# A graph network's attention ends: who weights the own rows, and where residual and bias are summed

## The reference

```
def gat_conv(x, src, dst, W, att_src, att_dst, bias, n_nodes):
    h = (x @ W).reshape(n_nodes, Hh, Cc)
    ...
    w = e / jnp.clip(denom, 1e-16)[dst]
    out = jax.ops.segment_sum(w[:, :, None] * h[src], dst, num_segments=n_nodes)
    return out.reshape(n_nodes, Hh * Cc) + bias
...
loops = jnp.arange(n, dtype=edge_index.dtype)
src = jnp.concatenate([edge_index[0], loops])
dst = jnp.concatenate([edge_index[1], loops])
h1 = gat_conv(x, src, dst, W1, att_src1, att_dst1, b1, n)
h1 = jax.nn.relu(h1)
out = gat_conv(h1, src, dst, W2, att_src2, att_dst2, b2, n)
...
x = x + _L1_gnn_ref(h, ...)
```

## Time and profile before

| | |
|---|---|
| median of three runs | 5653.39 us |
| the profiled execution, own time | 5650.82 us |
| its span in the profile | 5649.0 us |
| mean granted TensorE clock | 0.767 of full speed |
| PE busy | 4218.4 us (75%) |
| DVE busy | 3705.7 us (66%) |
| ACT busy | 2101.0 us (37%) |
| POOL busy | 4159.4 us (74%) |
| end of layer 0: first L699 to the last L1521's end | 4397.60 to 4463.94 us |
| end of layer 1: first L699 to the last L1772's end | 5563.05 to 5642.16 us |

### The profile page before, as it was taken

The page is one execution under the profiler, slowest core; times in us unless marked ns, Lnnn a source line. Parts: engine busy times, 40 slices in busy tenths (PEclk is TensorE's granted clock), DMA queues, the critical chain, the costliest instruction groups (busy, mean ns, idle before and its releaser), DMA issues.

```text
span 5649.0 us, 84292 instructions
## 1 busy us (share of the span) xinstructions
PE 4218.4 (75%) x14997; PEld 2470.4 (44%) x14997; DVE 3705.7 (66%) x12168; ACT 2101.0 (37%) x7038; POOL 4159.4 (74%) x4290
## 2 busy tenths in 40 slices
PE   8677777777777778677777777777777677777772
PEld 7433333343333335333333355555554455555551
DVE  7555555555555554555555568777777677777777
ACT  4000000020000003000000088888887688888881
POOL 8677777777777777777777747777776677777776
PEclk7777677787777668777777778878888888888886
DMA  2443333333333333433333354444444344444444
GB/s 94 117 111 106 106 105 106 105 108 106 106 105 105 105 106 100 131 105 105 106 106 106 106 167 110 110 110 110 110 111 125 99 110 110 110 110 110 110 112 151
DMA packets 309459, 625.61 MB, mean 111 GB/s; under 512 B 85044, under 2 KB 180264, under 8 KB 308937
## 3 DMA queue, kind: packets, MB, share of 16 engines
q0 software_dynamic: 192928, 530.18, 33.3%
q1 hardware_dynamic: 109656, 88.65, 5.0%
q10 hardware_dynamic: 6384, 1.39, 0.1%
HBM read 573.37 MB, written 47.33 MB: 110 GB/s over the span
## 4 chain that ended last, share of the span: by engine, by line
PE 40%; POOL 20%; DMA 14%; issue 11%; DVE 10%; ACT 5%; POOLq 0%; DVEq 0%; SPq 0%; ACTq 0%
PE main L1071 20%; POOL ring L667 13%; PE main L1174 11%; DMA ring<-conv_tab,csrc 9%; DMA ring<-attn_tab,sidx 5%; POOL ring L679 5%; DVE acc L1365 3%; PE main L990 3%; POOL ring L699 2%; PE pso L1094 2%; ACT ring L912 2%; DVE ring L1226 1%; ACT oh L890 1%; DVE ad L1584 1%; PE pso L982 1%
## 5 line engine op out<-in xcount | busy, mean ns | idle before, releaser
L667 POOL DMA_INDIRECT ring<-conv_tab,csrc x2346 | 2222.6, 947 | 749.2 <-issue 590.4
L1071 PE MATMUL main<-ring,oh 128*128 x4992 | 2207.0, 565 | 758.2 <-DVE acc L1365 325.1
L1365 DVE TENSOR_TENSOR acc<-acc,main 128x264 f32 (+2 forms) x4160 | 1761.8, 424 | 1254.2 <-PE main L1071 1157.6
L679 POOL DMA_INDIRECT ring<-attn_tab,sidx x1664 | 1590.8, 956 | 604.5 <-issue 361.7
L1071 PEld LDWEIGHTS main<-ring,oh 128*128 128x128 f32 x4992 | 1092.0, 259 | 1869.7 <-issue 1801.3
L1174 PE MATMUL main<-ring,oh 128*128 128x264 f32 x3328 | 1246.2, 491 | 120.6 <-ACT ring L912 69.2
L912 ACT ACTIVATE ring<-ring 128x64 f32<-128x64 f32 x3328 | 910.9, 343 | 0.0
L1357 DVE TENSOR_SCALAR oh<-iota,dloc 128x128 f32<-128x128 f32 x2505 | 814.8, 325 | 91.9 <-issue 79.6
L1174 PEld LDWEIGHTS main<-ring,oh 128*128 128x128 f32 x3328 | 619.3, 229 | 290.3 <-DVE ring L1690 222.8
L890 ACT ACTIVATE oh<-iota,dloc 128x128 f32<-128x128 f32 x1664 | 528.9, 394 | 3.4 <-DMA attn_tab<-oh 3.4
L1690 DVE TENSOR_TENSOR ring<-ring 128x128 f32<-128x128 f32 x1664 | 463.1, 284 | 0.0
(11 more groups left out here) (212 smaller groups left out, 2993.3 us busy)
## 6 DMA issues: line engine op xcount, KB each, us to landing
ring<-conv_tab,csrc POOLq DMA_INDIRECT x2346, 2.7
ring<-attn_tab,sidx POOLq DMA_INDIRECT x1664
ring<-attn_tab SPq DMA_DIRECT2D x14, 896.0 KB, 8.5
conv_tab<-oh SPq DMA_DIRECT2D x12, 896.0 KB, 4.0
flag_room<-start_rows SPq DMA_DIRECT2D x416, 8.0 KB
flag_room<-end_rows SPq DMA_DIRECT2D x416, 8.0 KB
x_tab<-acc SPq DMA_DIRECT2D x7, 896.0 KB
oh<-x_tab SPq DMA_DIRECT2D x7, 896.0 KB
```

The source lines that it names most:

```text
L667: pool.indirect_dma_start(ring3[:, c % U, 0:C], None, conv_tab[k], bass.IndirectOffsetOnAxis(ap=csrc[:, c:c + 1], axis=0)).then_inc(gather ...
L679: pool.indirect_dma_start(ring3[:, j, 0:TW], None, attn_tab[l], bass.IndirectOffsetOnAxis(ap=sidx[:, i * GB * G + j:i * GB * G + j + 1], a ...
L1071: nc.tensor.matmul(main[s % 4][:, 0:width], oh[:, (s % OHR) * P:(s % OHR + 1) * P], ring[:, bass.ds(slots[s % 8], width)], start=True, sto ...
L1365: nc.vector.tensor_tensor(a, a, main[k][:, 0:width], ALU.add).then_inc(added, 1)
```

## The change

Three edits.

1. Of the seven tiles of a block, ScalarE weights the last one at the end of layer 0 and the last three at the end of layer 1 (`OWN_BY_ACT`), with four instructions of 128 x 64 for each tile (`own_rows`). GpSimd weights the other six or four. VectorE's first pass over a block waits for both. At the end of layer 0 the instructions for blocks 0 and 1 stand ahead of ScalarE's first rectified tile, those for block i + 2 inside block i, ahead of its fourth round. At the end of layer 1 they stand behind everything else of ScalarE.
2. At the end of layer 1 TensorE sums the negated residual and the negated bias of a block in PSUM, in four parts of 512, 512, 512 and 256 columns: an identity matrix times the residual's rows, and a row of ones times a row that holds the negated bias twice. Even blocks use the four `main` banks, odd ones the other four. TensorE may begin block i when VectorE is done with block i - 2. VectorE makes the negated bias row with two instructions in the middle of layer 1.
3. VectorE's passes for bias and residual at the end of layer 1 (L1521, L1772) are replaced by four instructions which subtract the parts from PSUM. The last block's rows are stored with two DMAs instead of one: four tiles after its second part, the others after its fourth.

```
@@ store_result @@
             def store_result(q):
-                a, b = q * TB, min((q + 1) * TB, NFULL)
-                sp.wait_ge(mid_ready, 2 * NT + 2 * TB * (q + 1))
-                sp.dma_start(out[a * P:b * P, :]..., acc3[:, a:b, 0:C]).then_inc(stored, 16)
+                cuts = (0, TB) if q < NI - 1 else (0, 4, TB)
+                for a, b in zip(cuts, cuts[1:]):
+                    sp.wait_ge(mid_ready, 2 * NT + TB * q + b)
+                    a, b = q * TB + a, min(q * TB + b, NFULL)
+                    sp.dma_start(out[a * P:b * P, :]..., acc3[:, a:b, 0:C]).then_inc(stored, 16)
@@ gpsimd @@
-                    for j in range(TB):
+                    for j in range(TB - OWN_BY_ACT[l]):
@@ scalar @@
+            def own_rows(l, i):
+                if i == 0:
+                    act.wait_ge(nself, EC + l + 1)
+                act.wait_ge(row_block_in[i], 16 * (l + 3))
+                for t in range((i + 1) * TB - OWN_BY_ACT[l], (i + 1) * TB):
+                    for h in range(H):
+                        r = ring[:, t * C + h * CH:t * C + (h + 1) * CH]
+                        nc.scalar.activation(r, r, ACT.Copy, scale=es[:, t * H + h:t * H + h + 1]).then_inc(own_by_act, 1)
@@ rectify_last @@
+                own_rows(0, 0)
+                own_rows(0, 1)
                 one(0)
...
                 for t in range(NT):
+                    if t % TB == 3 and t // TB + 2 < NI:
+                        own_rows(0, t // TB + 2)
                     if t + 2 < NT:
                         one(t + 2)
@@ tensor, behind the last edge step @@
+            for i in range(NI):
...
+                if i >= 2:
+                    pe.wait_ge(mid_ready, 2 * NT + TB * (i - 1))
+                pe.wait_ge(x1_back[i % XB], X1_FROM + 16 * (i // XB + 1))
+                x1 = oh[:, i % XB * TB * C:(i % XB + 1) * TB * C]
+                for q in range(4):
+                    a, b = 2 * q * C, min(2 * q + 2, TB) * C
+                    nc.tensor.matmul(sums[i % 2][q][:, 0:b - a], ident[:, :], x1[:, a:b], start=True, stop=False)
+                    mm = nc.tensor.matmul(sums[i % 2][q][:, 0:b - a], ones[0:1, 0:P], tmp[0:1, 0:b - a],
+                                          start=False, stop=True)
+                mm.then_inc(x1_summed, 1)
@@ vector @@
-                for p in range(3):
-                    finish(i, p)
-                dve.wait_ge(mid_ready, i * 2 * TB + (2 * NT + TB))
-                dve.wait_ge(x1_back[i % XB], X1_FROM + 16 * (i // XB + 1))
...
-                nc.vector.tensor_tensor(a, a, x1, ALU.subtract).then_inc(mid_ready, TB)
+                finish(i, 0)
+                finish(i, 1)
+                dve.wait_ge(dve_chain, i * 2 + (chain[0] - 2 * NI + 2))
+                dve.wait_ge(x1_summed, X1_SUMMED_FROM + i + 1)
+                for q in range(4):
+                    a, n = i * TB + 2 * q, min(2, TB - 2 * q)
+                    rows = acc3[:, a:a + n, 0:C]
+                    nc.vector.tensor_tensor(rows, rows, sums_of_x1[i % 2][q][:, 0:n * C]..., ALU.subtract
+                                            ).then_inc(mid_ready, n)
```

More of the change, by code:

```diff
@@ L65 @@
 XB = 4
+OWN_BY_ACT = (1, 3)
 XE = 4
@@ L347, in gnn @@
         X1_FROM = FLAG_INCS * LAYERS * (NG // GB)
+        own_by_act, OWN_ACT_FROM = keys_ready, 1
+        x1_summed, X1_SUMMED_FROM = hist_onehots, 2 * NH
+        bias_row, BIAS_ROW = chunks_ready, 3
         weighted_v = sem("weighted_v")
@@ L559, in store_result @@
             def store_result(q):
-                a, b = q * TB, min((q + 1) * TB, NFULL)
-                sp.wait_ge(mid_ready, 2 * NT + 2 * TB * (q + 1))
-                sp.dma_start(out[a * P:b * P, :].rearrange("(t p) c -> p t c", p=P), acc3[:, a:b, 0:C]
-                             ).then_inc(stored, 16)
+                cuts = (0, TB) if q < NI - 1 else (0, 4, TB)
+                for a, b in zip(cuts, cuts[1:]):
+                    sp.wait_ge(mid_ready, 2 * NT + TB * q + b)
+                    a, b = q * TB + a, min(q * TB + b, NFULL)
+                    sp.dma_start(out[a * P:b * P, :].rearrange("(t p) c -> p t c", p=P), acc3[:, a:b, 0:C]
+                                 ).then_inc(stored, 16)
             def x1_rows(q):
@@ L590, in _ @@
             sp.dma_start(out[NFULL * P:N, :], acc3[0:NREST, NFULL, 0:C]).then_inc(stored, 16)
-            sp.wait_ge(stored, 16 * (2 * NI + 1))
+            sp.wait_ge(stored, 16 * (2 * NI + 2))
             sp.wait_ge(table_stored, 16 * NS * (HOPS + LAYERS))
@@ L954, in _ @@
                     rectify_last()
+                else:
+                    for i in range(NI):
+                        own_rows(l, i)
         @block.tensor
@@ L1192, in _ @@
                                     logit_step(n + (b + 2) * Q, tiles, j)
+            sums = (main, (pso[0], pso[1], psad, psb))
+            pe.wait_ge(bias_row, BIAS_ROW)
+            pe.wait_ge(added, 4 + (HOPS + LAYERS) * S)
+            for i in range(NI):
+                if i == 1:
+                    pe.wait_ge(ohT_copied, 2 + LAYERS * QT)
+                    pe.wait_ge(ad_ready, LAYERS * NG)
+                    pe.wait_ge(expo_ready, GB + LAYERS * NG)
+                    pe.wait_ge(factor_ready, LAYERS * NG)
+                if i >= 2:
[8 more added lines that the diff above has]
+                mm.then_inc(x1_summed, 1)
         @block.vector
@@ L1509, in part @@
                     if p == 0:
-                        dve.wait_ge(self_ready, l * NT + i * TB + TB)
+                        dve.wait_ge(self_ready, sum(NI * (TB - n) for n in OWN_BY_ACT[:l]) + (i + 1) * (TB - OWN_BY_ACT[l]))
+                        dve.wait_ge(own_by_act, OWN_ACT_FROM + H * (NI * sum(OWN_BY_ACT[:l]) + (i + 1) * OWN_BY_ACT[l]))
                         own = ring[:, bass.ds(i * TB * C, TB * C)].rearrange("p (t c) -> p t c", c=C)
@@ L1701, in _ @@
                         logit_columns(1)
+                    if l == 1 and it == 2:
+                        dve.wait_ge(bias_in, 16 * (l + 2))
+                        link(nc.vector.tensor_scalar(tmp[0:1, 0:C], bias[0:1, :], -1.0, None, ALU.mult))
+                        nc.vector.tensor_scalar(tmp[0:1, C:2 * C], bias[0:1, :], -1.0, None, ALU.mult).then_inc(bias_row, 1)
                     mark_base, marks[0] = chain[0], 0
@@ L1764, in _ @@
             finish = normalise(LAYERS - 1)
+            sums_of_x1 = (main, (pso[0], pso[1], psad, psb))
             for i in range(0, NI):
[L1766 to L1772 removed]
+                finish(i, 0)
[5 more added lines that the diff above has]
+                    rows = acc3[:, a:a + n, 0:C]
+                    nc.vector.tensor_tensor(rows, rows, sums_of_x1[i % 2][q][:, 0:n * C].rearrange("p (t c) -> p t c", c=C),
+                                            ALU.subtract).then_inc(mid_ready, n)
 _INS = ['x', 'src', 'dst', 'L0_gnn_W', 'L0_gnn_b', 'L1_gnn_W1', 'L1_gnn_att_src1', 'L1_gnn_att_dst1', 'L1_gnn_b1',
```

## The result

The changed kernel took 5668.93 us, median of nine runs (5662.19 to 5673.23), against 5653.39 us before (nine runs, 5647.58 to 5655.88): ratio 1.0028, 95% interval 1.0019 to 1.0037. It is slower by 15.5 us where 32 us less were forecast, and lies outside the range. The profiled execution took 5669.46 us, its span 5667.7.

The account below looks back on a forecast made before the run. POOL was taken to bound both layers' ends before, VectorE layer 1's end after. Layer 1's end -29.1, layer 0's end -3.5, bias row +0.4: -32.2 us from 5653.39, forecast 5621; range 5613 to 5632.

Parts of the forecast that it names:

- What bounds before, POOL and the passes: Both layers' ends: a POOL instruction takes 2.35 us under a VectorE pass, 0.57 otherwise; periods 11.1 and 9.34 us per block.
- Start of layer 1's end: Layer 1's end, block 0: the first VectorE pass starts at 5566.15 instead of 5567.22.
- VectorE's block and POOL beside the parts: Layer 1's end: four parts take 2.35 us, POOL running beside them; a block 7.25 us, 6.45 without POOL.
- beside: Layer 1's end: POOL's instructions run undisturbed beside VectorE's parts from PSUM; the value taken.
- waits as a pass does: Layer 1's end: each part waits for POOL, 1.2 us more per block; rival total 5626 us, chance 18%.
- TensorE's block: Layer 1's end: 16 instructions at full clock take 6.0 us per block, below VectorE's 7.25.
- a rival that got 5%: Layer 1's end: TensorE's clock stays at 1.2 GHz throughout, 12.0 us per block; total 5652.8 us, chance 5%.
- the rival "no change": Layer 1's end: TensorE at 1.2 GHz throughout bounds every block with 12.0 us; total 5652.8 us, chance 5%.
- The rival "slower": Layer 1's end: 1.2 GHz and each TensorE instruction waits for the previous; block 15.3 us, total 5676 us, chance 2%.
- Layer 0's end: POOL stays the bound with six tiles for seven, 8.77 us per block; -3.5 us, bounds -4.0 and -1.
- the lag that was feared: Layer 0's end: block 0 at 1.2 GHz may leave a lag, 0.5 us taken for it.
- Bias row, DMA and tail: Bias row in layer 1's edge steps +0.4 us; DMA no cost; tail after VectorE's end -1.4 us, bounds 0 and 2.

Follow-up runs that it names:

- eighth experiment: Changed kernel with the bias product on all 128 rows and GpSimd weighting all seven tiles again: 5626.44 us, ratio to before 0.9954.
- eleventh: The tenth experiment's kernel with ScalarE weighting six of seven tiles at layer 1's end in all blocks but the first: 5618.86 us, ratio to before 0.9939.
- ninth kernel: Changed kernel with the bias product an identity times the negated bias on all 128 rows, on an ordinary chip: 5622.63 us against 5654.52 before, ratio 0.9946.
- Experiments 1: Changed kernel with the bias product an identity times the negated bias on all 128 rows, on a slower chip: 6758.48 us, ratio to before 0.9945.
- third experiment: Changed kernel with the bias product on 128 rows of ones times 128 rows, 127 of them zero: 6758.80 us on a slower chip, ratio to before 0.9953.
- 5: The changed kernel again without any edit, on an ordinary chip: 5666.04 us against 5652.83 before, ratio 1.0024.
- 6: Changed kernel without TensorE's product of the residual, only the single-row bias products left: 5621.88 us (one run).
- second experiment: Changed kernel without the bias product, the identity times residual alone: 6754.88 us on a slower chip, ratio to before 0.9948.
- tenth experiment: The ninth kernel with ScalarE's four instructions per tile at layer 0's end spread over four rounds: 5619.78 us, ratio to before 0.9939.
- twelfth: Changed kernel with all rows for the bias product except a single row in the second part: 5631.90 us (one run), against 5658.69 before.

## Why the prediction was wrong, step by step

**What bounds before, POOL and the passes: right.** Periods of 11.1 and 9.34 us were built from 2.35 and 0.57 us, and the same two numbers gave the eighth experiment's 57 us (57.3) and the eleventh's 49.3 us.

**Start of layer 1's end: right.** The first pass began 4.52 us behind the reciprocal's start in every kernel with ScalarE's share, where before it was 5.63: 1.1 us earlier, as worked out.

**VectorE's block and POOL beside the parts: right, a little too dear.** The four parts take 2.13 us from the first's start to the next pass (5587.91 to 5590.04), where 2.35 was taken: 0.60 us from one part to the next in place of 0.69. The choice between "beside" and "waits as a pass does" came out as the earlier trace rows had it. In the ninth kernel the parts of block 0 last from 5570.18 to the next pass at 5572.31. Three of POOL's instructions overlap 5569.5 to 5571.6 (line L706):

```profile
L706 POOL TENSOR_TENSOR ring<-ring,es x3: 607/607/2389, 5568.2 to 5571.1; 128x256 f32<-128x256 f32 x3
```

Those that start in the parts take 607 ns, undisturbed; the one of 2389 ns started under the pass before. The parts are not lengthened either: the four last 2.21 us together here, and 2.21 us at 5597.45, where POOL is through. The Trainium skill, page "SBUF — State Buffer", section "Who interferes with whom", states both halves (two inputs in SBUF contend with a GpSimd instruction that reads there, one doesn't), and the trace agrees with both.

**TensorE's block: the step that failed.** "The clock at that place stands at 0.99 up to 5562 ... I take the full clock" and "6.0 us". That term was measured at 14.3 us. Both of its factors were wrong here:

- The clock. I argued from TensorE's busy share (83% against the projection's 91%) and named the single rows only under a rival that got 5%. Experiments 1, 3, 5, 6 and 9 settle it, in the same place of the program. With 128 rows in every product the clock is 1.0 at 90 to 100% busy, with real values or with zeros (but for a moment in the ninth); with single rows alone it is 0.50 at 92% busy; with the two taking turns it is 0.50 at 100% busy. Grouped, it goes up and down. The busy share in the profile doesn't tell how many rows work.
- The time per instruction. 0.43 us holds for products of 128 rows after one another. A change between 128 rows and one costs some 0.1 us on each side at 2.4 GHz, 0.13 to 0.16 at 1.2, and in the changed kernel every instruction stands beside such a change: 12 x 1.0 + 4 x 0.575 = 14.3 us a block. The first ones there, still at 1.0, show it: the second and third instruction, the two beside the first change, take 0.52 and 0.53 us from start to start (5561.25 to 5561.77 to 5562.31) instead of 0.43. The very first one's 0.50 is no sign of it, since it is 0.50 in the second experiment too, where nothing changes.

The size follows. The clock alone makes a block of 12.0 us; seven of them and the last parts, with the first instructions still at 1.0, come to about 84 us, +3 against the 80.6 before, the rival "no change" (its 5652.8 leaves out the bias row's 0.4). The changes add 7 x 2.3 = 16 us: +19.4 measured. The rival "slower" came nearest: blocks of 15.3 us for the 14.3 measured, layer 1's end +27.5 for +19.4, +23 in all for +15.5. Its first half, the low clock, was right. Its second, that each instruction waits for the one before because weights change, is true in part: an instruction beside a change is late, by 0.13 to 0.16 us at that clock, where the rival had 0.21 (1.06 against 0.85). The earlier trace rows speaks against it for weights of 128 rows alone. It got 2%, because I read rows 8 as speaking for weights of any kind.

With both mended, VectorE's end came 51.3 us behind the reciprocal's start, where the forecast was 5614.5 - 5561.6 = 52.9. So the rest of this stretch was right to 2 us. The ninth kernel, 5622.63, is 31.9 us faster than the kernel before beside it, where 32.2 were forecast. That this is so close is in part luck: the end was forecast 1.6 us too long, while layer 0's end and the tail gave 1.2 us less than forecast.

**Layer 0's end: right, with the lag that was feared.** POOL's part gave 3.98 us (the seventh block's first pass 57.60 us behind the reciprocal's start, 61.58 before). Of these 2.4 arrived. Timeline of ScalarE after, a round that the four instructions stand ahead of, then a block's head:

```profile
4443.69 1.05 ACT L871 ACTIVATE ring<-ring,es 128x64 f32<-128x64 f32 x4
4444.64 0.41 ACT L879 ACTIVATE nb<-acc 128x256 f32<-128x256 f32 x1
...
4446.55 0.39 ACT L811 ACTIVATE oh<-main 128x264 f32<-128x264 f32 x1 [0.39 <-PE main L1014]
...
4455.61 0.41 ACT L879 ACTIVATE nb<-acc 128x256 f32<-128x256 f32 x1
```

The round's head comes 0.95 us later, and at the head of block 5 (4455.61) ScalarE no longer waits for VectorE, where the earlier trace rows had 1.41 us: the cover of 0.17 us that I counted was used up. That the lag comes from block 0 and was never worked off is the likely reading, not a shown one. The tenth experiment takes the lag away and gets the whole 3.99.

**Bias row, DMA and tail: right within 0.5 us.** The residuals arrived in time: in the ninth kernel no engine waits for a DMA there. The tail lost 0.9 us, not 1.4.

**Open.** Where between one row and 128 the clock turns was not tried, nor a mix between one single-row product in eight (1.00 in the twelfth) and every second one (0.50), and why the change between the two kinds of weights costs time was not looked into.

## What to carry to other kernels

Before TensorE gets a pass of another engine, work out its time at 1.2 GHz too, and count the rows of the array that its products use, not the share of time it is busy. Products of a single row (a broadcast by a row of ones) are short to write, but each takes as long as a product of 128 rows with the same columns. They can hold the clock down for all others, and slow each neighbour that uses 128 rows. The same sum with an identity and all rows avoids it (end 51.3 us); putting the single-row ones together avoids most of it (56.9 us). Where an engine's instructions are to be taken over by one that runs a chain, spread them over the rounds: four at once cost 1.3 us of the 4.0 gained here in the ninth kernel, one in each round nothing in the tenth.

## What the runs showed of the hardware that was not expected

- Single-row full-precision products did not lift TensorE's clock: 0.50 at 92% busy when they run alone, 0.50 over 94 us at 100% busy when they take turns with products of 128 rows, 1.00 when the same columns use 128 rows of which 127 hold zeros.
- Changing between weights of 128 rows and of one costs TensorE 0.09 to 0.10 us before and after the change at 2.4 GHz, and 0.13 to 0.16 us at 1.2 GHz, while a change between two weight tiles of 128 rows costs nothing (0.86 us for two instructions of 512 columns, third experiment).
- Forecast, but seen in no row before: a VectorE instruction with one operand in PSUM and one in SBUF leaves GpSimd alone: 607 ns beside it, 2389 under one with both in SBUF.
